# Cross-attention with a routed expert layer: seven maxima blocks for eight, new orders of the matrix engine, the first bias on VectorE

## The chip, the cores and the metric

One core of one Trainium2 chip. The metric is the device time of one execution in microseconds (us). The engines are TensorE (PE; its weight loads are PEld), VectorE (DVE), ScalarE (ACT), GpSimd (POOL) and SyncE (SP), which here only issues DMAs. Each works through its own program in order and waits on semaphores.

## The reference

```python
# x (16, 224, 512), context (16, 750, 384); 16 heads of 32; 8 experts of width 256, top 2
x = x + cross_attention(layernorm(x), context)      # softmax(q k^T / sqrt(32)) v, then Wo, bo
n = layernorm(x)
logits = cosine(n, centroids) + n @ w_route.T
gates = softmax of the two largest logits
h = gelu(n @ w1[e] + b1[e], exact); y_e = h @ w2[e] + b2[e]
x = x + sum_e gates[e] * y_e
```

## The kernel before

**Attention.** A group is four heads of one batch element; there are 64 (`GROUPS`), four to a batch element, and a quarter (`first`, `second`, `third`, `fourth`) of each engine's program belongs to each of the four. In quarter g the matrix engine interleaves, in an order written out by hand (L1629 to L1769): the projections of Q and K for group g + 2, parts of V for the batch element, the maxima of the scores of group g + 1 (`score_for_max`, L1529), the scores of g in twelve pairs (`score`, L1551), their products with V (`values`, L1567, three steps), the denominators of g - 1 (L1584), and now and then the output projection, the transposes of x and y and the logits. The order of the shared PSUM banks `M` is computed from the same list (`misc_units`, L90).

The maxima: for every one of the 4 x 224 query rows of a group the maximum over 750 keys is needed ahead of the exponential. `score_for_max` multiplies a block of rows with all keys (two matmuls into the one buffer `X`), `maximum` (L1066) on VectorE reduces it. A block has 112 rows, so there are 8 (`XU`). `transpose_max` (L1544) turns the eight columns into rows, ScalarE negates them, a DMA puts them into `qst`, and `score` adds them by way of a row of ones.

Exponentials run on ScalarE into `pr` (two halves, L773); GpSimd adds the six key tiles in five steps (`add_step`, L478), and `denominators` sums over partitions. VectorE inverts (`invert`), ScalarE and VectorE split the result in a high and a low part, for the products of three (`split3`).

**Second layernorm.** `y_stats` (L1105) on VectorE; the reciprocal roots (of the variance and of the length) on GpSimd (`y_rsqrt`, L531, 16 instructions with `pow`); `y_apply` on ScalarE. `rsqrt` (L34) is the same root in 12 VectorE instructions, without `pow`.

**Weights of the experts.** Sixteen pieces are loaded by SP and split: ScalarE copies the high part, VectorE subtracts it (`w_part`, L1146), after groups 62 to 66 and once ahead of the table.

**Routing.** VectorE picks two experts for each token, computes slots (`place`), and builds with the matrix engine a table of token numbers for each slot (`find_columns`, `find_rows`). `table_done` lets the first gather start.

**Experts.** 63 tiles of 128 slots (`TILES`). GpSimd gathers the rows of tile i (`gather`) and adds the result to `out` (`add_rows`). On the matrix engine: `fold_x` (four transposes), `up` (one matmul of a row of ones with the two parts of b1, then twelve), `fold_h` (two transposes of the gelu's result), `down` (six). The loop's orders:

```
PE : fold_x(i+2)  up(i+1)    down(i)    fold_h(i+1)
ACT: x_high(i+2)  gelu(i+1)  h_high(i+1)  y_scale(i)
DVE: x_low(i+2)   y_bias(i)  (load of the expert number)  h_low(i+1)
```

`x_high` and `x_low` split x, `h_high` and `h_low` the hidden layer (`down` waits for `h_low`), `y_bias` adds b2 and `y_scale` applies the gate.

## Time and profile before

| | us |
|---|---|
| median of 3 runs | 1650.93 (1650.54 to 1652.68) |
| the profiled execution | 1648.43 |
| its span, first to last instruction | 1646.6 |
| PE booked | 1524.2 (93%) |
| DVE, ACT, POOL booked | 1030.6, 944.2, 1080.2 |
| mean granted clock of PE | 0.964 of full speed |

The attention lasts until about 1320 us, the expert loop begins at about 1403. An engine's booked time contains the drain of its instructions, so that a booked matrix engine is not one that streams. In a timeline, times are start and length in us; the idle time ahead of an instruction and what ended it stand in brackets.

### The profile page before, as it was taken

To read this page: it belongs to the slowest core of one execution; us is meant where nothing else is said; L and a number is where in the kernel's file an instruction comes from. 1 tells how busy PE (TensorE), PEld (TensorE's weight loads), DVE (VectorE), ACT (ScalarE), POOL (GpSimd) and SP (SyncE) were. 2 spreads that over 40 slices of the span, in tenths; PEclk is the share of its full clock that TensorE was granted. 3 is DMA by queue.
4 is the path that set the end of the run, shared out by engine and by line. 5 is a ranking of instruction groups with operands and counts; after the bars stand their busy time and mean duration, and the time that the engine had idled before them with its cause. 6 is when DMAs were issued, how large, how long until landed. Compare 5 with 4: busy or idle time off the path is not lost.

```text
span 1646.6 us, 33344 instructions
## 1 busy us (share of the span) xinstructions
PE 1524.2 (93%) x11534; PEld 1247.4 (76%) x11534; DVE 1030.6 (63%) x1475; ACT 944.2 (57%) x2055; POOL 1080.2 (66%) x931
## 2 busy tenths in 40 slices
PE   4899999999999999999999999999999743899997
PEld 4777777778787878787877877877777433798996
DVE  5556666666666676766666666666665568344443
ACT  4456666666666666666666666665665440455554
POOL 3366767676767677776676777777775740477675
PEclk9999999999999999999999999999999765899999
DMA  7556666666667676767666757676756733578785
GB/s 193 97 81 111 101 134 123 110 124 108 127 110 134 111 129 112 131 110 139 112 130 107 136 101 144 101 140 101 140 91 120 187 122 35 136 135 147 135 148 90
DMA packets 113394, 199.29 MB, mean 121 GB/s; under 512 B 20448, under 2 KB 49280, under 8 KB 113104
## 3 DMA queue, kind: packets, MB, share of 16 engines
q1 hardware_dynamic: 98992, 165.81, 54.4%
q0 software_dynamic: 14240, 31.35, 10.5%
q8 instruction: 98, 1.61, 0.5%
q14 instruction: 64, 0.52, 0.1%
HBM read 64.29 MB, written 38.66 MB: 63 GB/s over the span
## 4 chain that ended last, share of the span: by engine, by line
PE 86%; DVE 5%; ACT 3%; POOL 2%; issue 1%; DMA 1%; POOLq 0%; DVEq 0%; SPq 0%; ACTq 0%
PE M L320 12%; PE S L1563 12%; PE M L321 12%; PE M L322 12%; PE X L1540 11%; PE O L1579 10%; ACT pr L781 2%; PE M L1825 2%; PE X L1807 2%; PE X L1808 2%; PE X L1806 2%; PE M L1826 2%; PE M L1827 2%; PE M L1590 2%; PE S L1796 2%
## 5 line engine op out<-in xcount | busy, mean ns | idle before, releaser
L1072 DVE TENSOR_REDUCE mx<-X 112x1 f32<-112x752 f32 x512 | 480.6, 939 | 356.0 <-PE X L1540 353.9
L491 POOL TENSOR_TENSOR psum_p<-psum_p,pr 125x896 f32<-125x896 f32 x256 | 543.9, 2124 | 172.6 <-ACT pr L781 149.1
L781 ACT ACTIVATE pr<-S 125x448 f32<-125x448 f32 x768 | 395.0, 544 | 224.4 <-PE S L1563 216.6
L1563 PEld LDWEIGHTS S<-qst,kst 128*125 128x125 f32 x1536 | 234.7, 189 | 113.0 <-ACT pr L781 51.2
L1563 PE MATMUL S<-qst,kst 128*125 128x224 f32 x1536 | 287.3, 291 | 27.1 <-ACT pr L781 21.2
L1540 PE MATMUL X<-kh_s,q_own 128*112 128x376 f32 x1024 | 272.0, 347 | 8.4 <-DVE mx L1072 7.9
L1540 PEld LDWEIGHTS X<-kh_s,q_own 128*112 128x112 f32 x1024 | 153.9, 176 | 48.0 <-issue 26.8
L1579 PE MATMUL O<-pr,v 125*32 125x224 f32 x3072 | 188.6, 364 | 1.7 <-ACT pr L781 1.7
L488 POOL TENSOR_TENSOR psum_p<-pr 125x896 f32<-125x896 f32 x64 | 135.6, 2119 | 80.1 <-ACT pr L781 79.9
L475 POOL TENSOR_TENSOR ctx_l<-ctx_r,ctx_h 128x750 fp32r<-128x750 f32 x48 | 85.4, 1811 | 74.7 <-ACT ctx_h L696 74.7
L320 PE MATMUL M<-ctx_h,wk_h 128*128 128x376 f32 (+1 forms) x384 | 130.0, 339 | 0.0
L321 PE MATMUL M<-ctx_l,wk_h 128*128 128x376 f32 (+1 forms) x384 | 129.4, 337 | 0.0
L322 PE MATMUL M<-ctx_h,wk_l 128*128 128x376 f32 (+1 forms) x384 | 128.8, 335 | 0.0
L1579 PEld LDWEIGHTS O<-pr,v 125*32 125x32 f32 x3072 | 81.3, 110 | 62.3 <-issue 23.1
L662 POOL DMA_INDIRECT out<-y_out,table_t x63 | 99.9, 1586 | 41.4 <-ACT y_out L1003 23.3
L654 POOL DMA_INDIRECT xg<-rows_d,table_x x63 | 62.4, 990 | 86.3 <-DVE settled L1400 43.0
L320 PE MATMUL M<-wv_h,ctx_h 128*125 128x512 f32 x288 | 116.8, 405 | 0.0
L322 PE MATMUL M<-wv_h,ctx_l 128*125 128x512 f32 x288 | 113.6, 394 | 0.0
L321 PE MATMUL M<-wv_l,ctx_h 128*125 128x512 f32 x288 | 113.5, 394 | 0.0
L1079 DVE RECIPROCAL M<-M 128x224 f32<-128x224 f32 x64 | 99.8, 1559 | 21.7 <-PE M L1590 21.6
L738 ACT ACTIVATE q_own<-qh_s,own 128x224 fp32r<-128x224 f32 x256 | 102.6, 472 | 2.1
L1062 DVE SCALAR_TENSOR_TENSOR kl_s<-M,bk_s,kh_s 128x376 fp32r<-128x376 f32 (+1 forms) x128 | 77.0, 602 | 14.3 <-ACT kh_s L749 14.1
(222 smaller groups left out, 3005.1 us busy)
## 6 DMA issues: line engine op xcount, KB each, us to landing
kst<-kh_s SPq DMA_DIRECT2D x128, 375.0 KB, 7.3
kst<-kl_s SPq DMA_DIRECT2D x64, 375.0 KB, 10.4
ctx_r<-ctxT SPq DMA_DIRECT2D x48, 375.0 KB, 12.2
qst<-qh_s SPq DMA_DIRECT2D x128, 112.0 KB, 2.8
rows_d<-x_res SPq DMA_DIRECT2D x32, 448.0 KB, 10.6
w_l<-w SPq DMA_DIRECT2D x16, 512.0 KB, 7.0
x_ln<-x SPq DMA_DIRECT2D x17, 448.0 KB, 11.0
qst<-ql_s SPq DMA_DIRECT2D x64, 112.0 KB, 3.0
```

Of the source, the lines that this page charges most:

```text
L320: pe.matmul(out, lhs[0], rhs[0], start=first, stop=False)
L321: pe.matmul(out, lhs[0], rhs[1], start=False, stop=False)
L322: return pe.matmul(out, lhs[1], rhs[0], start=False, stop=last)
L488: pool.tensor_tensor(out=total, in0=tiles[0], in1=tiles[1], op=ALU.add).then_inc(sum_step, 1)
L491: pool.tensor_tensor(out=total, in0=total, in1=tiles[half], op=ALU.add).then_inc(sum_step, 1)
L662: pool.indirect_dma_start(out=out[:, :], out_offset=bass.IndirectOffsetOnAxis(ap=table_t[:, i:i + 1], axis=0), in_=y_out[:, i % YO, :], in ...
L738: act.activation(q_own[:, g % 2, j, :], qh_s[:, g % 2, :], ACT.Copy, scale=own[:, j:j + 1]).then_inc(own_done, 1)
L781: act.activation(pr[0:KP, (3 * g + p) % 2, j, :, :], S[0:KP, n % SB, 0:2 * NQ].rearrange("p (i n) -> p i n", i=2), ACT.Exp).then_inc(exp_d ...
L1072: dve.tensor_reduce(mx[0:QP, u:u + 1], X[0:QP, :, 0:HALF[0][1]], AX.XY, ALU.max).then_inc(max_done, 1)
L1540: last = pe.matmul(X[0:QP, i, 0:w], q_own[:, g % 2, j, QP * qt:QP * (qt + 1)], kh_s[:, g % 2, off:off + w], start=True, stop=True)
L1563: last = pe.matmul(S[0:KP, n % SB, NQ * h:NQ * (h + 1)], kst[:, i, j, o:o + KP], qst[:, i, j, :], start=True, stop=True)
L1579: last = pe.matmul(O[HD * j:HD * (j + 1), 0:NQ], v[0:KP, 2 * p + i, HD * j:HD * (j + 1)], pr[0:KP, (3 * g + p) % 2, j, i, :], start=(p == ...
```

## The change

- `XU` is 7: the rows of the four heads are taken as one row of 896 and cut in blocks of 128. All eighth calls of `score_for_max` and `maximum` go.
- The four orders of the matrix engine and `misc_units` are written anew. Two of the four are shown.
- The roots of batch elements 14 and 15 are computed on VectorE (`late_root`), with `rsqrt` twice. GpSimd's constants come one group later, and there are two fewer.
- The last group's denominators take three of the five additions and the two last exponential tiles directly.
- b1 is written to DRAM and read back as a broadcast to all partitions; VectorE adds it (`h_bias`) ahead of the gelu, and the matmul with ones goes.
- b2 is loaded after the last output projection, not after the table.
- The weight subtractions on VectorE are dealt out otherwise: 2 after group 63 (5 before), 4 after 64 (3), 4 after 66 (4), 3 behind the table (1 ahead of it).
- `hot_row` is a ring of three chunks, not four.
- The expert loop's orders are new on three engines; x is prepared three tiles ahead.

```diff
-XU = 8
+XU = GH * NQ // P
...
-LN_STEPS, Y_STEPS = 8, 16
+LN_STEPS, Y_STEPS, LATE_STEPS = 8, 16, 2 * RSQRT_STEPS + 3
+LATE = B - 2
...
+ROWS = 3 * CHUNK
...
+        def roots(b):
+            return Y_STEPS * min(b, LATE) + LATE_STEPS * max(0, b - LATE)
+
+        def shifted(b):
+            return roots(b) + (LN_STEPS if b < LATE else RSQRT_STEPS + 1)
...
-                    if not 0 <= g < GROUPS:
+                    if not 0 <= g < GROUPS or (g == GROUPS - 1 and i >= 3):
...
-                        sp.wait_ge(zeroed, 1)
-                        sp.wait_ge(b1_hi, 1)
-                        sp.dma_start(b1_hl[0:1, :, :].bitcast(F32), b1_th[:, :].bitcast(F32)).then_inc(b1_both, 16)
-                        sp.wait_ge(b1_lo, 1)
-                        sp.dma_start(b1_hl[1:2, :, :].bitcast(F32), b1_tl[:, :].bitcast(F32)).then_inc(b1_both, 16)
+                        sp.wait_ge(b1_out, 1)
+                        sp.dma_start(b1_d[:, :], b1_t[:, :]).then_inc(b1_flat, 16)
                         sp.wait_ge(s_full, 12 * GROUPS)
                         load_pieces(E + 2, 2 * E)
+                        sp.wait_ge(b1_flat, 16)
+                        sp.dma_start(b1_all[:, :, :], b1_d.rearrange("(a e) p -> a (e p)", a=1).rearrange("a (e n) -> a e n", n=DE)
+                                     .broadcast_to([P, E, DE])).then_inc(b1_in, 16)
                     if t == 2 and b + 2 < B:
...
+                wait_full(sp, "O1", B - 1)
+                sp.dma_start(b2_all[:, :, :], b2.rearrange("(a e) n -> a e n", a=1).broadcast_to([P, E, D])
+                             ).then_inc(b2_in, 16)
                 sp.wait_ge(route, 15)
                 for i in range(2):
                     sp.dma_start(gates_of[i], gate4[0:QP, :, i, :]).then_inc(gate_out, 16)
-                sp.wait_ge(table_done, 1)
-                sp.dma_start(b2_all[:, :, :], b2.rearrange("(a e) n -> a e n", a=1).broadcast_to([P, E, D])
-                             ).then_inc(b2_in, 16)
-
                 sp.wait_ge(need_done, 1)
                 for i in range(1, TILES):
...
-                    if not 0 <= b < B:
+                    if not 0 <= b < LATE:
...
-                        act.wait_ge(sum_step, 5 * GROUPS)
-                        act.wait_ge(b1_both, 32)
+                        wait_full(act, "den", GROUPS - 1)
+                        act.wait_ge(b1_flat, 16)
...
-                    act.wait_ge(h_full, i + 1)
+                    act.wait_ge(h_read, i + 1)
                     if i >= 2:
                         act.wait_ge(ht_full, i - 1)
-                    act.activation(hid[:, i % 2, :], HP[:, i % 2, 0:DE], ACT.Gelu).then_inc(gelu_done, 1)
+                    act.activation(hid[:, i % 2, :], h_raw[:, i % 2, :], ACT.Gelu).then_inc(gelu_done, 1)
...
                 gelu(0)
+                x_high(2)
                 h_high(0)
                 for i in range(TILES):
-                    if i + 2 < TILES:
-                        x_high(i + 2)
                     if i + 1 < TILES:
                         gelu(i + 1)
+                    if i + 3 < TILES:
+                        x_high(i + 3)
+                    y_scale(i)
+                    if i + 1 < TILES:
                         h_high(i + 1)
-                    y_scale(i)
...
+                def late_root(b):
+                    n, m = roots(b), mv2[0:QP, :, :]
+                    v, y, tmp, off = ve2[0:QP, :], rstd2[0:QP, :], rtmp2[0:QP, :], shift2[0:QP, :]
+                    sq, ln = square[0:QP, :], length[0:QP, :]
+                    dve.wait_ge(y_var, QT * (b + 1))
+                    dve.wait_ge(yn_done, QT * b)
+                    rsqrt(dve, newton2, n, m[:, :, 1], EPS, ALU.add, v, y, tmp)
+                    n += RSQRT_STEPS
+                    dve.scalar_tensor_tensor(out=off, in0=m[:, :, 0], scalar=-1.0, in1=y, op0=ALU.mult,
+                                             op1=ALU.mult).then_inc(newton2, 1)
+                    wait_free(dve, "lg1", b - 1)
+                    dve.tensor_tensor(out=sq, in0=m[:, :, 1], in1=y, op=ALU.mult).then_inc(newton2, 1)
+                    dve.wait_ge(newton2, n + 2)
+                    dve.scalar_tensor_tensor(out=sq, in0=sq, scalar=float(D), in1=y, op0=ALU.mult,
+                                             op1=ALU.mult).then_inc(newton2, 1)
+                    dve.wait_ge(newton2, n + 3)
+                    rsqrt(dve, newton2, n + 3, sq, NORM_EPS2, ALU.max, v, ln, tmp)
+
...
+                    if b >= LATE:
+                        late_root(b)
...
-                        dve.wait_ge(b1_hi, 1)
-                        dve.tensor_tensor(out=b1_tl[:, :], in0=HP[0:2 * E, 0, 0:P], in1=b1_th[:, :],
-                                          op=ALU.subtract).then_inc(b1_lo, 1)
-                        for n in range(3, E):
+                        for n in range(3, 5):
                             w_part(n)
                     if g == GROUPS:
-                        for n in range(E, E + 3):
+                        for n in range(5, E + 1):
                             w_part(n)
                     if g == GROUPS + 2:
-                        dve.wait_ge(made, 8)
+                        dve.wait_ge(made, 7)
                         dve.tensor_scalar(upper[:, :], iota[:, :], float(DUMP + 1), lane[:, 0:1], ALU.add,
                                           ALU.is_gt).then_inc(masks, 1)
-                        dve.wait_ge(newton2, Y_STEPS * B)
-                        for n in range(E + 3, 2 * E - 1):
+                        for n in range(E + 1, E + 5):
...
-                w_part(2 * E - 1)
...
+                for n in range(E + 5, 2 * E):
+                    w_part(n)
...
+                def h_bias(i, e):
+                    dve.wait_ge(h_full, i + 1)
+                    if i >= 2:
+                        dve.wait_ge(gelu_done, i - 1)
+                    dve.tensor_tensor(out=h_raw[:, i % 2, :], in0=HP[:, i % 2, 0:DE], in1=b1_all[:, e, :],
+                                      op=ALU.add).then_inc(h_read, 1)
...
                 x_low(0)
                 e = expert_of(0)
                 x_low(1)
+                dve.wait_ge(b1_in, 16)
+                h_bias(0, e)
+                x_low(2)
                 h_low(0)
                 dve.wait_ge(b2_in, 16)
                 for i in range(TILES):
-                    if i + 2 < TILES:
-                        x_low(i + 2)
+                    if i + 1 < TILES:
+                        after = expert_of(i + 1)
+                        h_bias(i + 1, after)
+                    if i + 3 < TILES:
+                        x_low(i + 3)
                     y_bias(i, e)
                     if i + 1 < TILES:
-                        e = expert_of(i + 1)
                         h_low(i + 1)
+                        e = after
...
                         return
-                    j, qt = u // QT, u % QT
+                    own_q = q_own[:, g % 2, :, :].rearrange("p j n -> p (j n)")
                     if u == 0:
                         pe.wait_ge(kh_done, 2 * (g + 1))
-                    if qt == 0:
-                        pe.wait_ge(own_done, GH * g + j + 1)
+                    pe.wait_ge(own_done, GH * g + (P * (u + 1) - 1) // NQ + 1)
                     if g or u:
                         pe.wait_ge(max_done, XU * g + u)
                     for i, (off, w) in enumerate(HALF):
-                        last = pe.matmul(X[0:QP, i, 0:w], q_own[:, g % 2, j, QP * qt:QP * (qt + 1)],
+                        last = pe.matmul(X[:, i, 0:w], own_q[:, P * u:P * (u + 1)],
                                          kh_s[:, g % 2, off:off + w], start=True, stop=True)
                     last.then_inc(x_full, 1)
...
-                    pe.wait_ge(sum_step, 5 * (g + 1))
-                    for j in range(GH):
-                        last = pe.matmul(out[HD * j:HD * (j + 1), 0:NQ], ones[0:KP, :], psum_p[0:KP, g % 2, j, :],
-                                         start=True, stop=True)
+                    parts = [psum_p[0:KP, g % 2, :, :]]
+                    if g == GROUPS - 1:
+                        pe.wait_ge(sum_step, 5 * g + 3)
+                        pe.wait_ge(exp_done, 12 * (g + 1))
+                        parts += [pr[0:KP, (3 * g + 2) % 2, :, h, :] for h in range(2)]
+                    else:
+                        pe.wait_ge(sum_step, 5 * (g + 1))
+                    for n, part in enumerate(parts):
+                        for j in range(GH):
+                            last = pe.matmul(out[HD * j:HD * (j + 1), 0:NQ], ones[0:KP, :], part[:, j, :],
+                                             start=n == 0, stop=n == len(parts) - 1)
                     last.then_inc(full, 1)
...
                 def third(g, b):
                     project_q(g + 2)
                     score_for_max(g + 1, 0)
+                    values(g - 1, 2)
+                    score_for_max(g + 1, 1)
                     project_k(g + 2, 0)
-                    score_for_max(g + 1, 1)
-                    score(g, 0)
-                    values(g - 1, 2)
-                    score(g, 1)
-                    score_for_max(g + 1, 2)
-                    project_k(g + 2, 1)
-                    score(g, 2)
-                    score_for_max(g + 1, 3)
                     project_v(b + 1, 0, 0)
                     project_v(b + 1, 0, 1)
+                    score(g, 0)
+                    score_for_max(g + 1, 2)
+                    score(g, 1)
+                    score(g, 2)
+                    project_k(g + 2, 1)
                     score(g, 3)
+                    score_for_max(g + 1, 3)
+                    score(g, 4)
+                    score(g, 5)
                     denominators(g - 1)
+                    values(g, 0)
                     score_for_max(g + 1, 4)
                     project_v(b + 1, 1, 0)
-                    score(g, 4)
-                    score(g, 5)
                     project_v(b + 1, 1, 1)
                     score_for_max(g + 1, 5)
-                    values(g, 0)
                     score(g, 6)
+                    score(g, 7)
                     score_for_max(g + 1, 6)
-                    score(g, 7)
                     score(g, 8)
                     score(g, 9)
-                    score_for_max(g + 1, 7)
                     values(g, 1)
                     score(g, 10)
                     transpose_max(g + 1)
...
                 def fourth(g, b):
                     score_for_max(g + 1, 0)
                     project_q(g + 2)
+                    project_k(g + 2, 0)
+                    score_for_max(g + 1, 1)
                     values(g - 1, 2)
-                    score_for_max(g + 1, 1)
-                    project_k(g + 2, 0)
+                    score(g, 0)
                     score_for_max(g + 1, 2)
-                    score(g, 0)
                     score(g, 1)
                     project_k(g + 2, 1)
+                    score_for_max(g + 1, 3)
                     score(g, 2)
-                    score_for_max(g + 1, 3)
+                    score(g, 3)
+                    project_v(b + 1, 2, 0)
                     denominators(g - 1)
-                    project_v(b + 1, 2, 0)
-                    score(g, 3)
                     project_v(b + 1, 2, 1)
+                    score(g, 4)
+                    project_v(b + 1, 3, 0)
+                    score(g, 5)
+                    project_v(b + 1, 3, 1)
                     score_for_max(g + 1, 4)
-                    score(g, 4)
-                    score(g, 5)
-                    project_v(b + 1, 3, 0)
-                    project_v(b + 1, 3, 1)
-                    score_for_max(g + 1, 5)
                     score(g, 6)
                     score(g, 7)
+                    score_for_max(g + 1, 5)
                     values(g, 0)
-                    score_for_max(g + 1, 6)
-                    values(g, 1)
                     score(g, 8)
                     score(g, 9)
                     transpose_y(b - 1, 0)
                     transpose_y(b - 1, 1)
-                    score_for_max(g + 1, 7)
+                    score_for_max(g + 1, 6)
+                    values(g, 1)
                     score(g, 10)
                     transpose_max(g + 1)
                     score(g, 11)
...
-                        pe.wait_ge(gelu_done, i - 1)
+                        pe.wait_ge(h_read, i - 1)
                     h = HP[:, i % 2, 0:DE]
-                    pe.matmul(h, ones_r[:, :], b1_hl[:, e, :], start=True, stop=False)
                     for c in range(DC):
-                        pe.matmul(h, xTs[:, 0, i % 2, c, :], w1_h[:, e, c, :], start=False, stop=False)
...
-                pe.wait_ge(b1_both, 32)
-                pe.wait_ge(ew_lo, W_PIECES)
                 fold_x(0)
                 fold_x(1)
                 e = expert_of(0)
                 up(0, e)
+                fold_x(2)
                 fold_h(0)
                 for i in range(TILES):
-                    if i + 2 < TILES:
-                        fold_x(i + 2)
                     if i + 1 < TILES:
                         after = expert_of(i + 1)
                         up(i + 1, after)
+                    if i + 3 < TILES:
+                        fold_x(i + 3)
                     down(i, e)
                     if i + 1 < TILES:
                         fold_h(i + 1)
...
```

## Rows read from the trace of the kernel before

**Rows 1.** The page, chain that ended last, by engine

```profile
PE 86%; DVE 5%; ACT 3%; POOL 2%; issue 1%; DMA 1%; POOLq 0%; DVEq 0%; SPq 0%; ACTq 0%
```

**Rows 2.** Stretches, sum over one batch element: us, then booked us of each engine

```profile
sum 79.26, PE 78.01 PEld 62.82 DVE 52.66 ACT 49.47 POOL 56.35; mean PE 19.50 PEld 15.71 DVE 13.16 ACT 12.37 POOL 14.09
```

**Rows 3.** Chain in order of time, 700 to 704 us: start, us, what

```profile
701.02 0.43 PE S L1563 x4
701.46 0.89 PE O L1579 x16
...
702.76 0.34 PE X L1540 x2
```

**Rows 4.** Timeline of PE, end of a fourth quarter

```profile
764.19 0.57 PE L1540 MATMUL X<-kh_s,q_own 128*112 128x376 f32 x2
...
765.92 0.26 PE L1549 MATMUL M<-id_s,mx 112*8 112x112 f32 x1
```

**Rows 5.** Timeline of PE, one tile of the expert loop

```profile
1560.30 0.36 PE L1804 MATMUL X<-b_hl,ones_r 128*128 x1
1560.50 0.27 PE L1806 MATMUL X<-w_h,xTs 128*128 x1
...
1561.92 0.39 PE L1825 MATMUL M<-w_h,hTs 128*128 x1
...
1563.90 0.36 PE L1804 MATMUL X<-b_hl,ones_r 128*128 x1
```

**Rows 6.** Timelines of DVE, ACT and PE, pairs of instructions that follow one another

```profile
1560.03 0.69 DVE L1420 TENSOR_TENSOR y_raw<-M,b_all 128x512 f32<-128x512 f32 x1 [0.95 <-PE M L1827]
1560.69 0.42 DVE L1409 TENSOR_TENSOR hTs<-M,hTs 128x256 fp32r<-128x256 f32 x1
...
1563.63 0.69 DVE L1420 TENSOR_TENSOR y_raw<-M,b_all 128x512 f32<-128x512 f32 x1 [0.94 <-PE M L1827]
...
1565.60 0.69 DVE L1404 TENSOR_TENSOR xTs<-S,xTs 128x512 fp32r<-128x512 f32 x1 [0.54 <-ACT xTs L983]
...
1564.36 0.72 ACT L1003 ACTIVATE y_out<-y_raw,xg 128x512 f32<-128x512 f32 x1 [0.23 <-DVE y_raw L1420]
1564.99 0.58 ACT L983 ACTIVATE xTs<-S 128x512 fp32r<-128x512 f32 x1
...
1410.37 0.39 ACT L996 ACTIVATE hTs<-O 128x256 fp32r<-128x256 f32 x1 [0.78 <-PE O L1816]
...
1410.79 0.42 DVE L1409 TENSOR_TENSOR hTs<-O,hTs 128x256 fp32r<-128x256 f32 x1 [3.94 <-ACT hTs L996]
...
1636.82 0.42 DVE L1409 TENSOR_TENSOR hTs<-O,hTs 128x256 fp32r<-128x256 f32 x1
...
1637.37 0.47 PE L1825 MATMUL M<-w_h,hTs 128*128 x1 [1.14 <-DVE hTs L1409]
```

**Rows 7.** Waits, whole span: who waited for what, us in total, times, longest

```profile
DVE hTs L1409 <- issue: 7.6, 16, 1.0
```

**Rows 8.** Chain in order of time, between the loops

```profile
1307.56 1.08 POOL ve L539
...
1315.92 2.07 POOL psum_p L488
...
1321.51 8.20 DVE w_l L1149 x4
...
1395.90 7.29 DMA xg<-rows_d,table_x
```

**Rows 9.** Timeline of DVE, the root of the centroids' lengths

```profile
17.30 1.71 DVE L46 SCALAR_TENSOR_TENSOR ctmp<-ctmp,cve 8x1 f32<-8x1 f32 x1
19.04 0.15 DVE L47 SCALAR_TENSOR_TENSOR cinv<-ctmp,cinv 8x1 f32<-8x1 f32 x1
```

**Rows 10.** Stretches of 5 us: booked us (x instructions) of PE, PEld, DVE, ACT, POOL; PEclk, DMA

```profile
1280.00:1285.00 5.00, 3.05 (x17) 2.10 (x16) 3.47 (x4) 1.45 (x4) 5.00 (x4) 1.00 0.02 5
1285.00:1290.00 5.00, 4.22 (x27) 2.68 (x28) 0.99 (x2) 1.77 (x4) 2.68 (x2) 0.66 0.87 164
```

137 lines of the change are left out of this document (72 added, 65 removed).

## The prediction

> **What bounds the kernel now.** I read the stretches first, then the chain, then each engine's timeline. The chain that ended last runs for 86% of its length over the matrix engine [rows 1]. In a steady batch of the attention (four groups, 79.3 us) that engine is booked for 78.0 us [rows 2], and in the expert loop its instructions follow one another without a gap [rows 5]. So its instruction stream sets both loops; VectorE (52.7 of 79.3) and GpSimd (56.4) have room. Booked is not streaming, though: the timeline has the transpose of the maxima 1.73 us after the last maxima block (two matmuls of `score_for_max`), although only a score pair stands between them [rows 4]. There is one buffer `X`, and a block can't be followed by anything that needs its reduction before that time. Between the loops, from about 1282 to 1403 us, chains over VectorE, GpSimd and DMA decide.
>
> **Attention: eight maxima blocks become seven.** The same 896 query rows go through in blocks of 128 instead of 112. Each group loses one block of two matmuls of 376 columns, 0.34 us on the matrix engine [rows 3]; 63 of the 64 groups lie where it is the bound: 63 x 0.34 = 21 us. VectorE also loses a reduction, worth nothing by itself. The Trainium skill (TensorE: Matmul & The Clock Gate, Back-to-back issue gap) gives 376 / 2.4 + 2.5 = 159 ns a matmul, so 20 us here; the row has 170, so the trace nearly agrees.
>
> **New orders.** What they change is the distance between maxima blocks. A score pair takes 0.21 us and a value step 0.89 [rows 3]. In the third quarter before, three score pairs stand between two blocks: 0.34 + 0.63 = 0.97 us against 1.73, 0.8 us idle; in the fourth, one pair stands ahead of the transpose: 0.55 against 1.73, 1.2 us idle [rows 3, 4]. The new fourth puts a value step there and loses nothing; but it has two score pairs alone between blocks 4 and 5, and the new third between 5 and 6: 0.34 + 0.42 = 0.76 against 1.73, so 0.9 to 1.0 us twice, and `values` alone between blocks 0 and 1 of the third, another 0.3 to 0.5. Old idle about 2.0 us a batch, new 2.1 to 2.4: a tie, and I take zero. Its bounds are the whole idle time removed, 16 batches x 0.8 = -13 us, and half of the saving lost, +10. Attention: -21, from -34 to -11.
>
> **The first bias on VectorE.** The matmul with ones goes out of `up`. It holds 0.20 us of the 3.60 us of a tile [rows 5], so 3.40 are left (1.42 of them `up`). If the matrix engine stayed the bound, that would be -62 x 0.20 = -12 us. It doesn't stay the bound, because two engines get a new order. ScalarE now has gelu(i+1), x_high(i+3), y_scale(i), h_high(i+1); before, h_high(i+1) stood ahead of y_scale(i). VectorE has h_bias(i+1), x_low(i+3), y_bias(i), h_low(i+1). Engines work in program order, so h_high(i+1) is queued behind y_scale(i), which waits for y_bias(i), which waits for down(i); and down(i+1) waits for h_low(i+1), which waits for h_high(i+1). I follow that ring from start to start with the lags of the trace [rows 5, 6]:
> down(i) to y_bias(i) 1.71; to y_scale(i) 0.73; to the next ScalarE instruction 0.63; h_high to h_low 0.42; h_low to down(i+1) 0.55. Sum 4.04 us, more than the 3.60 of now. Before, the ring left out the middle pair: 1.71 + 0.66 + 0.55 = 2.92, and was hidden.
> A second ring needs no matrix engine, because all eight instructions of the two engines alternate: h_bias to gelu 0.46 (its 0.42, by h_low of the same width, and the 0.04 that y_bias to y_scale shows beyond 0.69); gelu to x_high 0.30 (0.39 less the 0.1 by which y_scale's successor starts before its end); x_high to x_low 0.61; x_low to y_bias 0.66 (as y_bias to h_low); y_bias to y_scale 0.73; y_scale to h_high 0.63; h_high to h_low 0.42; h_low to the next h_bias 0.38 (0.42 less the same overlap that y_bias to h_low shows). Sum 4.19 us [rows 6].
> In that last step VectorE also loads the expert's number into a register. Now the load stands behind y_bias, whose 0.66 us cover it except in 16 of the 63 tiles, which waited 7.6 us in all [rows 7]. Behind h_low only 0.38 cover it: 0.12 us a tile at least, and at most 0.28 more. I take 0.18 in all: 4.37 us a tile. From that 62 x (4.37 - 3.60) = +48 us; the ends are 4.04 (+27) and 4.60 (+62). Prefetching three tiles ahead instead of two gives nothing where these rings decide. GpSimd's gather and scatter of a tile keep pace with 3.60 us now and so with more.
>
> **Between the loops.** (a) `y_rsqrt(14)` and the constants leave GpSimd, where they stand for 8.4 us ahead of the last group's sums [rows 8]. Two of the last group's five additions go as well: its denominators take the third pair of exponentials directly, for 8 more short matmuls. Perfectly used, this and the four weight subtractions of 2.05 us that hold up `invert(63)` [rows 8] are worth about 10 us. (b) But the roots go to VectorE as a chain of 27 small instructions, 21 of them with two SBUF operands, ahead of three weight subtractions and of `invert(62)`; behind that stands `o_hi(62)` on ScalarE, and behind it the exponentials of the last group. Beside GpSimd's subtractions such a tiny instruction (8x1) took 1.71 us, where others of its kind took 0.15 [rows 9]. The Trainium skill says so (GPSIMD Engine Reference, Key points): GpSimd shares its SBUF interfaces with VectorE, in contention with two-input instructions. The trace agrees by those rows, and it speaks against this move. GpSimd's sums of group 62 end at 1307.5 us [rows 8]; with four or five such stalls until then and 0.2 us (0.15 and the hand-over) for each of the other steps, the chain takes 4 x 1.7 + 17 x 0.2 = about 10 us. VectorE has some 2 us to spare there, by my estimate, so `invert(62)` comes some 8 us later, and most of the gain of (a) is eaten: I take -3 us, between -9 and +4. The root of batch 15 meets an idle GpSimd: 13 steps of 0.2 us to the shift, against 2.7 us now, no change. (c) One weight subtraction leaves the chain ahead of the table and three go behind it, under the first gather: -1 (0 to -2). (d) `b2` (2 MB) is no longer issued with the first gather, which took 7.3 us [rows 8]: -1.5 (0 to -3). (e) The first bias goes through DRAM and back as a broadcast, far ahead of the loop; three row buffers instead of four and the shorter waits are hidden by PE's own work there. Sum -5.5, from -14 to +4.
>
> **The sum.** -21 + 48 - 5.5 = +21.5 us on the profiled execution's 1648.4 us: 1670. The median of the runs shown is 2.5 us above it; I leave the forecast at 1670.
>
> **Rivals.** (A) The loop of experts stays with the matrix engine, as if y_scale found its data early: 3.40 to 3.60 us a tile. Then 1648.4 - 21 - 5.5 - 6 = 1616. Against it: y_scale starts 0.73 us after y_bias, which starts 1.71 after down, as the rows have it [rows 5, 6]. That leaves an error in my reading of the orders, or buffers that let the engines drift; 12%.
> (B) The rings are as short as their lower end, 4.04 us, and the new orders of the attention take out all idle time: -34 + 27 - 9 = -16, 1632. It is faster than before, the other side from my forecast, and is decided by whether the second ring's VectorE part (h_bias behind h_low, x_low ahead of y_bias) is really serial. 7% for a result below 1647.
> (C) Attention and transition give nearly as much as the rings take: within 0.2%; 5%.
> (D) The gap of about a microsecond in each tile costs clock: from 1280 to 1285 us the engine was booked for 3.05 of 5 us, and in the next 5 us the granted clock was 0.66 of full speed, so partly at 1.2 GHz instead of 2.4 [rows 10]. In the loop it would be at work for 3.40 of 4.37 us. A tile at the lower level holds up to 6.8 us of matrix work, 2.4 more than the ring; one tile in six so would be 10 x 2.4 = +24, 1694. 12%.
> Forecast itself: 64%, its own range 1648 to 1692.
>
> **Numbers.** 1670 us; the range that leaves no more than 2 in 10 out: 1630 to 1698. Faster by over 0.2% (3.3 us, about what a measurement can tell from no change) 0.19, same 0.05, slower 0.76.
>
> **What would show it.** Right: down to down 4.2 to 4.6 us in the expert loop, matrix engine waiting for h_low there, ScalarE's y_scale directly ahead of h_high with no idle time of note on VectorE or ScalarE; a batch of the attention at 77.9 us (1.4 less), with waits of PE for `mx` between score pairs of the third and fourth quarter; in the transition small root instructions of 1.7 to 2.1 us on VectorE. Wrong: tiles at 3.4 to 3.6 us (the rings are not closed), a batch under 77 us (orders worth more than the block), a transition shortened by over 10 us (no contention).

## The result, and the profile after it

The changed kernel takes 1692.36 us (median of 4 runs, 1691.41 to 1694.39), the one before 1651.44 us beside it (4 runs): ratio 1.0242, 95% interval 1.0228 to 1.0255, slower by 41 us. The forecast was 1670, with a range of 1630 to 1698: the sign and the mechanism of the loop were right, the size of the loss was put at half of what it is. The page's header, its chain by engine (it answers to [rows 1]) and its clock:

```profile
span 1690.5 us, 33260 instructions
...
PEclk9999999999999999999999999999997659999999
...
PE 64%; DVE 12%; issue 11%; ACT 6%; POOL 4%; DVEq 1%; DMA 1%; ACTq 0%; POOLq 0%; SPq 0%
```

The matrix engine's part of the chain fell from 86 to 64%; VectorE's rose from 5 to 12%, and "issue", time in which an engine waited for nothing that the profile shows, from 1 to 11%. The two spans, 1646.6 and 1690.5 us, cut at marks that both timelines have (the transposes of the maxima, and the first matmul of each tile's `down`):

| stretch | before, us | after, us | difference | forecast |
|---|---|---|---|---|
| start to the last transpose of maxima (attention) | 1299.0 | 1284.3 | -14.7 | -21 |
| to the first `down` (between the loops) | 113.7 | 109.2 | -4.5 | -5.5 |
| first to last `down` (62 tiles) | 224.7 | 287.8 | +63.1 | +48 |
| to the end | 9.2 | 9.2 | 0 | 0 |
| sum | 1646.6 | 1690.5 | +43.9 | +21.5 |

So the loop of experts is the whole loss: 4.64 us a tile (median 4.61) where it was 3.62. The timelines of VectorE, then of ScalarE, then of the matrix engine, for one tile of it (start, us of work, engine, line, what, in brackets the idle time ahead and who ended it); they answer to [rows 5, 6]:

```profile
1504.26 0.42 DVE L1450 TENSOR_TENSOR hTs<-O,hTs 128x256 fp32r<-128x256 f32 x1 [1.06 <-ACT hTs L1014]
1505.08 0.42 DVE L1445 TENSOR_TENSOR h_raw<-X,b_all 128x256 f32<-128x256 f32 x1 [0.39 <-issue]
1506.47 0.69 DVE L1438 TENSOR_TENSOR xTs<-S,xTs 128x512 fp32r<-128x512 f32 x1 [0.97 <-ACT xTs L1001]
1507.08 0.68 DVE L1461 TENSOR_TENSOR y_raw<-M,b_all 128x512 f32<-128x512 f32 x1
1508.82 0.42 DVE L1450 TENSOR_TENSOR hTs<-M,hTs 128x256 fp32r<-128x256 f32 x1 [1.06 <-ACT hTs L1014]
1509.76 0.42 DVE L1445 TENSOR_TENSOR h_raw<-X,b_all 128x256 f32<-128x256 f32 x1 [0.51 <-issue]
```

```profile
1505.54 0.42 ACT L1008 ACTIVATE hid<-h_raw 128x256 f32<-128x256 f32 x1 [1.31 <-DVE h_raw L1445]
1505.86 0.58 ACT L1001 ACTIVATE xTs<-S 128x512 fp32r<-128x512 f32 x1
1507.80 0.72 ACT L1021 ACTIVATE y_out<-y_raw,xg 128x512 f32<-128x512 f32 x1 [1.36 <-DVE y_raw L1461]
1508.42 0.36 ACT L1014 ACTIVATE hTs<-M 128x256 fp32r<-128x256 f32 x1
```

```profile
1504.82 0.47 PE L1873 MATMUL M<-w_h,hTs 128*128 x1 [0.39 <-DVE hTs L1450]
...
1509.38 0.47 PE L1873 MATMUL M<-w_h,hTs 128*128 x1 [0.40 <-DVE hTs L1450]
```

Read the first two side by side and the second ring of the forecast stands there, each instruction started by the one before it on the other engine: `h_bias` 1505.08, `gelu` 1505.54, `x_high` 1505.86, `x_low` 1506.47, `y_bias` 1507.08, `y_scale` 1507.80, `h_high` 1508.42, `h_low` 1508.82, the next `h_bias` 1509.76. Both engines idle for over half of the time (VectorE is booked for 110 of 240 us, ScalarE for 97, below), each waiting for the other in turn, and the matrix engine waits for `h_low` in every tile. The lags are 0.46, 0.32, 0.61, 0.61, 0.72, 0.62, 0.40 and 0.94 us. The waits of the whole span say the same of all tiles (us in total, times, longest); the second line answers to [rows 7]:

```profile
DVE hTs L1450 <- ACT hTs L1014: 65.8, 62, 1.1
...
DVE h_raw L1445 <- issue: 30.3, 61, 1.0
...
PE M L1873 <- DVE hTs L1450: 26.8, 62, 2.2
...
PE X L1854 <- issue: 16.1, 61, 0.4
```

"issue" ahead of `h_raw` is VectorE's register load of the expert's number, and what `h_bias` itself has to pass behind it: half a microsecond in 61 tiles, where [rows 7] have it in 16 for 7.6 us. The granted clock of the whole stretch was 1.00, the level of 2.4 GHz, with the matrix engine booked for 205 of 240 us (columns: stretch, length, busy us and count of PE, PEld, DVE, ACT and POOL, clock, DMA share, GB/s):

```profile
1420.00:1660.00 240.00, 205.21 (x1231) 164.43 (x1230) 109.90 (x206) 96.93 (x205) 132.23 (x103) 1.00 0.62 109
```

In the attention, a steady batch (stretches, sum; it answers to [rows 2]) and the matrix engine's timeline at the two places that the forecast named (third quarter, blocks 5 to 6; fourth, blocks 4 to 5) and at the fourth's transpose, which answers to [rows 4]:

```profile
sum 78.31, PE 76.00 PEld 62.07 DVE 47.01 ACT 48.68 POOL 56.26; mean PE 76.00 PEld 62.07 DVE 47.01 ACT 48.68 POOL 56.26
```

```profile
812.90 0.50 PE L1586 MATMUL X<-kh_s,q_own 128*128 128x376 f32 x2
813.24 0.59 PE L1609 MATMUL S<-qst,kst 128*125 128x224 f32 x4
814.52 0.58 PE L1586 MATMUL X<-kh_s,q_own 128*128 128x376 f32 x2 [0.70 <-DVE mx L1092]
...
830.18 0.51 PE L1586 MATMUL X<-kh_s,q_own 128*128 128x376 f32 x2
831.82 0.59 PE L1586 MATMUL X<-kh_s,q_own 128*128 128x376 f32 x2 [0.69 <-DVE mx L1092]
...
834.47 0.59 PE L1586 MATMUL X<-kh_s,q_own 128*128 128x376 f32 x2
...
836.20 0.27 PE L1595 MATMUL M<-id_s,mx 128*7 128x128 f32 x1
```

Ahead of the last line, the transpose, nothing is idle any more: the value step fills the time. Two waits of 0.7 us stand where the forecast put 0.9 to 1.0.

### The profile page after: what moved, and what is told of

Same layout as the page of the kernel before. It is cut to its first block, busy times and chain, and to the rows that moved or that the text cites. A ratio compares the mean times of both kernels' runs of the same rounds, so it can differ in the third digit from the quotient of the medians.

```text
span 1690.5 us, 33260 instructions
## 1 busy us (share of the span) xinstructions
PE 1512.7 (89%) x11359; PEld 1229.2 (73%) x11359; DVE 975.4 (58%) x1527; ACT 926.2 (55%) x2055; POOL 1062.6 (63%) x895
## 4 chain that ended last, share of the span: by engine, by line
PE 64%; DVE 12%; issue 11%; ACT 6%; POOL 4%; DVEq 1%; DMA 1%; ACTq 0%; POOLq 0%; SPq 0%
PE M L343 11%; PE M L345 11%; PE M L344 11%; PE S L1609 10%; PE X L1586 9%; PE O L1625 8%; POOL psum_p L513 3%; DVE y_raw L1461 2%; DVE mx L1092 2%; PE M L1643 2%; ACT pr L799 2%; DVE h_raw L1445 1%; ACT hTs L1014 1%; DVE hTs L1450 1%; ACT xTs L1001 1%
## 5 line engine op out<-in xcount | busy, mean ns | idle before, releaser
L1092 DVE TENSOR_REDUCE mx<-X 128x1 f32<-128x752 f32 x448 | 421.1, 940 | 441.7 <-PE X L1586 440.2
L513 POOL TENSOR_TENSOR psum_p<-psum_p,pr 125x896 f32<-125x896 f32 x254 | 537.1, 2115 | 179.5 <-ACT pr L799 156.6
L799 ACT ACTIVATE pr<-S 125x448 f32<-125x448 f32 x768 | 385.7, 543 | 222.5 <-PE S L1609 192.8
L1609 PEld LDWEIGHTS S<-qst,kst 128*125 128x125 f32 x1536 | 241.9, 190 | 89.5 <-ACT pr L799 42.3
L1586 PE MATMUL X<-kh_s,q_own 128*128 128x376 f32 x896 | 241.4, 351 | 31.9 <-DVE mx L1092 27.4
L1586 PEld LDWEIGHTS X<-kh_s,q_own 128*128 128x128 f32 x896 | 145.3, 191 | 68.8 <-issue 49.4
L1625 PE MATMUL O<-pr,v 125*32 125x224 f32 x3072 | 183.9, 361 | 2.5 <-ACT pr L799 2.5
L1625 PEld LDWEIGHTS O<-pr,v 125*32 125x32 f32 x3072 | 85.3, 110 | 59.9 <-issue 18.1
L344 PE MATMUL M<-wv_l,ctx_h 128*125 128x512 f32 x288 | 113.7, 395 | 0.0
L1021 ACT ACTIVATE y_out<-y_raw,xg 128x512 f32<-128x512 f32 x63 | 45.6, 724 | 87.2 <-DVE y_raw L1461 80.4
```

The source lines that it names most:

```text
L344: pe.matmul(out, lhs[0], rhs[1], start=False, stop=False)
L513: pool.tensor_tensor(out=total, in0=total, in1=tiles[half], op=ALU.add).then_inc(sum_step, 1)
L799: act.activation(pr[0:KP, (3 * g + p) % 2, j, :, :], S[0:KP, n % SB, 0:2 * NQ].rearrange("p (i n) -> p i n", i=2), ACT.Exp).then_inc(exp_d ...
L1092: dve.tensor_reduce(mx[:, u:u + 1], X[:, :, 0:HALF[0][1]], AX.XY, ALU.max).then_inc(max_done, 1)
L1586: last = pe.matmul(X[:, i, 0:w], own_q[:, P * u:P * (u + 1)], kh_s[:, g % 2, off:off + w], start=True, stop=True)
L1609: last = pe.matmul(S[0:KP, n % SB, NQ * h:NQ * (h + 1)], kst[:, i, j, o:o + KP], qst[:, i, j, :], start=True, stop=True)
```

## The experiments

Four questions: is it the ring, and what is its register load worth; what bounds the loop once the ring is open; where the attention's saving stayed; and what the move of the roots costs. All kernels are the changed one with an edit, except where the text says that the base is the kernel before. Ratios are to the kernel before, on the same chip; where fewer than four runs stand behind a time, their number is given.

### The ring: `e1_gate_last`, `e2_load_early`, `e3_both`

The first gives ScalarE the order of before for two instructions:

```diff
-                    y_scale(i)
                     if i + 1 < TILES:
                         h_high(i + 1)
+                    y_scale(i)
```

> The changed kernel with one line moved: on ScalarE h_high(i+1) stands ahead of y_scale(i) again. Theory (two closed rings set the expert loop): without y_scale both rings open; what is left is h_bias to gelu 0.46, to x_high 0.32, to x_low 0.61, to y_bias 0.61, to h_low 0.65, and 0.88 to the next h_bias with its register load = 3.53 us a tile instead of 4.64, so 62 x 1.11 = 69 us less: about 1624 us. Rival (the loop is slow because the bias went to VectorE at all, or because of the prefetch three tiles ahead, and the place of y_scale is immaterial): 4.4 to 4.6 us a tile, 1680 to 1692 us.

Measured: 1636.96 us (2 runs), ratio 0.9903 (0.9875 to 0.9932), 3.765 us a tile (median 3.64). Two lines exchanged are worth 55 us: with `h_high(i+1)` ahead of `y_scale(i)` neither ring closes. The tile isn't at 3.53 us, though, as was expected.

The second moves only VectorE's register load, to behind `y_bias(i)`, an expert earlier:

```diff
                     if i + 1 < TILES:
-                        after = expert_of(i + 1)
                         h_bias(i + 1, after)
...
                     y_bias(i, e)
+                    e = after
+                    if i + 2 < TILES:
+                        after = expert_of(i + 2)
```

> The changed kernel with only VectorE's load of the expert number moved: the number of tile i+2 is loaded behind y_bias(i), not ahead of h_bias(i+1). Theory (the register load costs about 0.5 us in every tile when only 0.38 us of h_low cover it): h_low to h_bias falls from 0.82 to 0.94 us to 0.38, the ring to 4.64 - 0.50 = 4.14 us, 62 x 0.5 = 31 us less: about 1661 us. Rival (the gap ahead of h_bias is not the load but a wait for the matrix engine's up): no change, 1690 to 1694 us.

Measured: 1661.16 us (4 runs), ratio 1.0042 (1.0017 to 1.0066), 4.10 us a tile, as expected (1661 us, 4.14). The ring is whole here, but from `h_low` to `h_bias` it takes 0.34 us instead of 0.82 to 0.94. VectorE's timeline of this kernel:

```profile
1506.14 0.42 DVE L1450 TENSOR_TENSOR hTs<-M,hTs 128x256 fp32r<-128x256 f32 x1 [1.06 <-ACT hTs L1014]
1506.48 0.41 DVE L1445 TENSOR_TENSOR h_raw<-X,b_all 128x256 f32<-128x256 f32 x1
```

The ring without the load is 4.10 us (forecast 4.19), the load adds 0.54 (forecast 0.18). This settles the term that was mis-sized.

The third has both edits:

> Both edits. Theory: no ring over 3.2 us is left, the matrix engine is the bound again with 3.40 us a tile, or up to 3.7 if its own register load ahead of up stays visible (it waited 0.3 us there in the changed kernel): 62 x 0.95 to 1.25 = 59 to 77 us less, 1615 to 1633 us. Rival (the bias on VectorE costs the loop something by itself): over 3.75 us a tile, over 1637 us.

Measured: 1637.54 us, ratio 0.9907 (0.9878 to 0.9936), 3.73 us a tile, no different from the first. That lies between the 3.70 us of the theory and the 3.75 of the rival, and decides between them no more than the time does. So the two cures don't add up: with the ring open VectorE has time for its load, and something else holds the tile at 3.7 us. A candidate was the matrix engine's own register load between `fold_h` and `up` ("PE X L1854 <- issue" in the waits above, of the change). In this kernel, too, the start of `up` lies later behind the last transpose of `fold_h` than it need: 0.17 us by the median and up to 0.58 in nine tiles of ten, where it is 0.03 in the kernels that have that load elsewhere.

### What bounds the open loop: `e5_loads`, `e10_pe_load`

`e5_loads` is `e3_both` with that load put where the matrix engine has queued work, behind `fold_x(i + 3)` and ahead of `down`, an expert earlier:

```diff
                     if i + 1 < TILES:
-                        after = expert_of(i + 1)
                         up(i + 1, after)
                     if i + 3 < TILES:
                         fold_x(i + 3)
-                    down(i, e)
+                    e = after
+                    if i + 2 < TILES:
+                        after = expert_of(i + 2)
+                    down(i, now)
```

> The kernel with both edits of the loop (gate scaling behind h_high, VectorE's load early), and the matrix engine's load of the expert number moved too: the number of tile i+2 is loaded behind fold_x(i+3), ahead of down(i), instead of between fold_h and up. Theory (the 0.3 to 0.6 us that the matrix engine idles between fold_h and up are this load): 3.40 to 3.50 us a tile instead of 3.73, 62 x 0.28 = 17 us less: about 1620 us. Rival (up waits there for something else, such as x_low): no change, 1634 to 1640 us.

Measured: 1626.54 us (2 runs), ratio 0.9872 (0.9842 to 0.9902); median tile 3.48 us, mean 3.59. The median is the 3.40 to 3.50 of the theory, the mean isn't. With the bias still on VectorE the loop is now faster than that of the kernel before, so the rival of `e3_both` (the bias costs the loop something by itself) falls as well. In its timeline the matrix engine has no wait over many tiles, and in the stretch below it is booked for 176.5 of 180 us (`e3_both` for 176.4, so that the booked share doesn't tell the two apart):

```profile
1420.00:1600.00 180.00, 176.47 (x1200) 158.28 (x1199) 103.64 (x201) 101.08 (x200) 127.14 (x99) 1.00 0.77 139
```

This is the state in which the removed matmul of 0.20 us counts: 3.61 us (median of before) became 3.48. What separates mean and median are seven tiles of 3.8 to 5.4 us. GpSimd's waits name a possible part of it: its scatter of a tile was held by SP seven times, 14.6 us in all. That this is what makes these tiles late isn't shown.

`e10_pe_load` leaves VectorE's load where the change put it and has the two other edits:

> The changed kernel with h_high ahead of y_scale and with the matrix engine's register load moved, but VectorE's register load left where the change put it, between h_low and h_bias. My theory: once the ring over y_scale is open, VectorE is no longer the bound and its load costs next to nothing: e1_gate_last's 3.765 us a tile less the 0.14 that the moved load of the matrix engine gave between e3_both and e5_loads, so 3.62 us, 1628 us. Rival: VectorE's four instructions and its load are themselves the bound as soon as the matrix engine's idle time is gone: no gain over e1_gate_last, 3.73 to 3.77 us, 1635 to 1637 us.

Measured: 1632.09 us (4 runs), ratio 0.9882 (0.9865 to 0.9898); 3.634 us a tile, median 3.48. The tile is as my theory had it (3.62), and not at the rival's 3.73 to 3.77; the time is 4 us above the theory's 1628. The same register load that cost 0.54 us a tile inside the ring costs 0.04 outside of it by the means and nothing by the medians (3.48 in both); `e9_loads_gaps` (below), which has the loop of `e5_loads` line for line, has a mean of 3.66, so that 0.04 isn't told from nothing. Of the 6.1 us between the profiled executions of `e10_pe_load` and `e5_loads`, 2.7 lie in the loop and 3.6 in the attention, where one of the last groups alone took 4.5 us more (below).

### Where the attention's saving stayed: `e4_gaps`, `e7_seven_old_orders`, `e8_old_orders_loads`, `e9_loads_gaps`

`e4_gaps` puts longer work between the maxima blocks that wait:

```diff
 in third:
-                    score_for_max(g + 1, 1)
                     project_k(g + 2, 0)
+                    score_for_max(g + 1, 1)
...
                     denominators(g - 1)
-                    values(g, 0)
                     score_for_max(g + 1, 4)
...
                     score(g, 7)
+                    values(g, 0)
                     score_for_max(g + 1, 6)
 in fourth:
-                    score_for_max(g + 1, 5)
                     values(g, 0)
+                    score_for_max(g + 1, 5)
```

> The changed kernel with three swaps in the matrix engine's orders of the attention: in the third quarter block 1 stands behind project_k and values(g, 0) between the score pairs 6, 7 and block 6; in the fourth values(g, 0) stands ahead of block 5. No two blocks are then closer than 1.4 us of work. Theory (these three places idle 0.4, 0.7 and 0.7 us a batch because X is still read by the reduction): 1.3 to 1.8 us less a batch, 16 batches, 20 to 29 us less: about 1668 us. Rival (the matrix engine would wait for exponentials or GpSimd's sums instead): under 6 us less, 1686 to 1692 us.

Measured: 1686.43 us, ratio 1.0203 (1.0173 to 1.0232): 6 us less than the change. A batch takes 78.06 us (sum of the four quarters' medians; 78.55 in the change), 0.5 less and not 1.3 to 1.8. The timelines of the matrix engine and of VectorE in the third quarter show why:

```profile
807.01 0.58 PE L1586 MATMUL X<-kh_s,q_own 128*128 128x376 f32 x2 [0.43 <-DVE mx L1092]
```

```profile
804.03 1.57 DVE L1099 RECIPROCAL M<-M 128x224 f32<-128x224 f32 x1
805.63 0.39 DVE L1106 TENSOR_TENSOR o_s<-o_s,M 128x224 f32<-128x224 f32 x1
805.93 0.93 DVE L1092 TENSOR_REDUCE mx<-X 128x1 f32<-128x752 f32 x1
```

The reduction of block 4 is now queued behind the reciprocal and the product of another group, 2 us, so block 5 waits for it. A gap filled in the matrix engine's order opened one in VectorE's, which I had not laid beside it. Over 700 to 860 us, two batches, the waits for the maxima are down to 0.9 us from the 2.8 of the change (below), so 0.95 a batch were won; half a microsecond of it goes to a wait that the change doesn't have, of the transposes of y for ScalarE:

```profile
PE M L1514 <- ACT x_res L830: 1.0, 2, 0.5
```

`e7_seven_old_orders` is the kernel before with seven blocks of 128 rows, its orders kept, block 7 left out of them:

```diff
-XU = 8
+XU = GH * NQ // P
...
 in each quarter:
-                    score_for_max(g + 1, 7)
```

> The kernel before with seven blocks of 128 rows and nothing else of the change: the eighth block's calls are struck out of the old orders. Theory (the new orders gave back part of what the block saved: idle time at the buffer X, which in the old orders stood mostly around block 7 of the third and fourth quarter, 0.7 and 1.2 us a batch, and goes with it): a batch of four groups takes 79.2 - 1.4 - 1.0 to 1.9 = 76 to 77 us, 16 batches, 35 to 50 us less than before: about 1608 us. Rival (the idle time moves to the score pairs and stays): 77.9 to 78.5 us a batch as in the changed kernel, 1630 to 1639 us.

Measured: 1637.45 us (3 runs), ratio 0.9935 (0.9896 to 0.9975). Counted over the same 60 groups (first transpose of maxima to the 61st): 1190.9 us before, 1180.7 here, 1177.9 in the change. The 0.34 us of a block, 20.4 us in 60 groups, are thus half kept with the old orders (5 of the 10 us in the first batch alone), and the new ones are worth 2.8 us more, where the seven kernels with the change's attention lie between 1177.8 and 1179.5. What takes up the other half here isn't the buffer `X`. The matrix engine's waits, in the same two batches (700 to 860 us), of the kernel before, of this one and of the change:

```profile
PE S L1563 <- ACT pr L781: 2.0, 4, 0.8
```

```profile
PE S L1558 <- ACT pr L781: 2.7, 4, 1.2
PE M L1585 <- POOL psum_p L491: 1.2, 3, 0.8
```

```profile
PE X L1586 <- DVE mx L1092: 2.8, 4, 0.7
PE S L1609 <- ACT pr L799: 0.9, 4, 0.3
PE X L1586 <- ACT q_own L756: 0.6, 2, 0.3
PE M L1643 <- POOL psum_p L513: 0.3, 1, 0.3
```

With the old orders the score pairs wait for ScalarE's exponentials and the denominators for GpSimd's sums: 3.9 us in two batches against 2.0 before, so 0.95 a batch more. Four blocks are 1.36 us; 1.36 - 0.95 leaves 0.4, and 0.5 was measured (79.22 to 78.73 us a batch by the quarters' medians). In the change the waits for the exponentials fall to 0.9 and those for the maxima and `q_own` come to 3.4, 4.6 us in all. By the same account only 0.1 us a batch would be left, where 0.7 is measured (78.55), so its orders also took out time to which no wait of before is put down: the matrix engine is booked for 76.0 us of a batch instead of 78.0 [rows 2], which is more than the 1.36 of the blocks.

The first of these lists has no wait of a matmul for the maxima (weight loads waited for them for 0.7 us in the two batches), and that bears on the forecast. Between the two lines of [rows 4] stands this one:

```profile
765.61 0.48 PE L1563 MATMUL S<-qst,kst 128*125 128x224 f32 x2 [0.84 <-ACT pr L781]
```

The idle time ahead of the transpose, which the forecast put down to the buffer `X`, stands ahead of a score pair that waits for one of ScalarE's exponentials. The reduction ended at 765.74 us, so the transpose couldn't have come much sooner either: the gap has two causes, and a block less takes away one of them.

`e8_old_orders_loads` has the old orders and the loop of `e5_loads`:

```diff
 e5_loads, in each quarter and in the planner's list:
-  the change's order
+  the order of before, without score_for_max(g + 1, 7)
```

> The changed kernel with the loop of e5 and the old orders of the attention less block 7. Theory (attention and expert loop are additive): the attention of e7 and the loop of e5, 1650 - 42 - 5 - 11 = about 1590 us. Rival (the old orders don't suit the changed kernel): the batch stays at 78.5 us, 1620 us.

Measured: 1635.01 us, ratio 0.9923 (0.9894 to 0.9952), against 1626.54 (0.9872) for `e5_loads`: neither my 1590 nor quite the rival. The 60 groups take 1183.3 us with the old orders and 1178.5 with the new. This fells the thought that the change's orders lose what the old ones would keep.

`e9_loads_gaps` adds the three swaps of `e4_gaps` to `e5_loads`:

> The three cures of the loop (as in e5_loads) together with the three swaps in the third and fourth quarter (as in e4_gaps). If the two add up, as they should, because they lie in different loops: a batch of the attention 0.5 us shorter, 8 us in all, and the loop at 3.59 us a tile: 1626.5 - 8 = 1619 us, ratio to the kernel before 0.981 to 0.983. If the swaps' saving falls among what other waits take up again: 1624 to 1627.

Measured: 1624.35 us (4 runs), ratio 0.9836 (0.982 to 0.9852), the fastest of all by its ratio, though the intervals of the two overlap. The 60 groups take 1172.4 us, 6.1 less than in `e5_loads`, as expected, but the profiled spans are equal (1625.8 and 1625.7): the last three groups give back 2.4 us and the loop 4 (a few more late tiles). The second last group is worth a look. In the seven kernels with the change's orders it takes from 19.25 to 23.80 us, here 20.65 and in `e4_gaps` 23.86. `e10_pe_load` is the one with 23.80; the matrix engine's timeline in it:

```profile
1257.11 0.45 PE L1609 MATMUL S<-qst,kst 128*125 128x224 f32 x2 [3.21 <-DMA qst<-mneg]
```

The score pair waits for the transfer of the maxima, which SP had issued at 1250.02, 7 us earlier. So the 3.6 us of attention between `e10_pe_load` and `e5_loads` are this group's, and `e4_gaps` lost in it over half of the 7.7 us that its swaps had gained in the 60 groups. It isn't the experts' weights that delay the maxima: the first of them is issued 23 us later,

```profile
1280.56 3.09 SPq L436 DMA_DIRECT2D w_l<-w  x3
```

What is under way are loads of x, of 448 KB each, issued at 1247.78 and 1248.14, and the copies of q and k. The second load of x lands 8.2 us after its issue, in `e5_loads`, where SP issues the same transfers in the same order, 5.5 us. Why the transfers are slower in one execution than in the other stays open.

### The roots: `e6_roots_pool`

```diff
-LATE = B - 2
+LATE = B
```

The last two batches' roots stay on GpSimd; all else is the change's.

> The changed kernel with LATE = B: all roots on GpSimd as before, nothing else. Theory (on VectorE the root of batch 14 is held up by GpSimd's additions and delays invert(62), and with it the last exponentials and ScalarE's eight weight copies behind them, more than its six us on GpSimd cost): last exponentials some 5 us earlier, about 6 us less: 1686 us. Rival (GpSimd's chain of additions decides, so that taking the roots off it was worth 6 us): 4 to 6 us more, 1697 us.

Measured: 1691.81 us (2 runs, 1688.73 and 1694.89), ratio 1.0268 (1.0216 to 1.032), the stretch between the loops 108.4 us against 109.2: no difference in the time. But two differences are in it that cancel. The timelines of VectorE, of the change (the same stretch of the transition) and then of this kernel; the last transpose of maxima, from which the times below are counted, is at 1284.3 us in the first and at 1288.2 in the second:

```profile
1283.94 1.18 DVE L41 TENSOR_SCALAR ve<-mv 112x2 f32<-112x2 f32 x1
...
1285.56 2.09 DVE L45 TENSOR_TENSOR rtmp<-rstd 112x2 f32<-112x2 f32 x1
1287.68 0.16 DVE L46 SCALAR_TENSOR_TENSOR rtmp<-rtmp,ve 112x2 f32<-112x2 f32 x1
1287.88 1.99 DVE L47 SCALAR_TENSOR_TENSOR rstd<-rtmp,rstd 112x2 f32<-112x2 f32 x1
...
1293.91 5.38 DVE L1189 TENSOR_TENSOR w_l<-w_l,w_h 128x1024 fp32r<-128x1024 f32 x3
1299.21 1.55 DVE L1099 RECIPROCAL M<-M 128x224 f32<-128x224 f32 x1
```

```profile
1291.19 1.65 DVE L1189 TENSOR_TENSOR w_l<-w_l,w_h 128x1024 fp32r<-128x1024 f32 x1 [3.42 <-ACT w_h L864]
...
1298.27 1.57 DVE L1099 RECIPROCAL M<-M 128x224 f32<-128x224 f32 x1 [1.25 <-PE M L1643]
```

The chain of roots of batch 14 takes 10 us on VectorE, with two stalls of 2.0 to 2.1 us and one of 1.2 (four or five of 1.7 were forecast). Without it `invert(62)` starts 10.1 us behind the last transpose instead of 14.9, so 4.9 us earlier, and the last exponentials end 4.8 us earlier, as the theory had it (5). The last output projection is still 4.8 us earlier. Then batch 15 takes the gain back. From its variance to `y_apply` it is 2.6 us in the change and 7.2 here, because GpSimd's first instruction of that root lasts as long as VectorE's four weight subtractions beside it:

```profile
1329.18 4.71 POOL L561 TENSOR_SCALAR ve<-mv 112x2 f32<-112x2 f32 x1 [15.49 <-DVE mv L1154]
```

```profile
1329.18 4.62 DVE L1189 TENSOR_TENSOR w_l<-w_l,w_h 128x1024 fp32r<-128x1024 f32 x4
```

The kernel before had VectorE wait for that root ahead of the subtractions (`dve.wait_ge(newton2, Y_STEPS * B)` in the diff); the change took that wait out, and this kernel doesn't put it back. So the run doesn't price the move of both roots against the order of before. It shows that batch 14's root costs 4.8 us on VectorE, and that batch 15's would cost 4.6 us on GpSimd without the wait; batch 14 on GpSimd and batch 15 on VectorE together wasn't run.

## Why the prediction was right in its sign and short in its size

**The ring, right.** The forecast followed the two engines' orders round and found a closed ring of eight instructions, 4.19 us with lags of the trace before; seven of its lags sum to 3.81 in the forecast and 3.74 in the trace after, and `e2_load_early` measured 4.10 for the whole. The first ring, 4.04, was the shorter of the two and didn't decide: from `down` to `y_bias` it has 2.26 us (1504.82 to 1507.08) instead of 1.71. `e1_gate_last` shows the cause by itself, 55 us for one exchange.

**The register load, wrong: the term that was mis-sized.** "I take 0.18 in all" became 0.54: 62 x 0.36 = 22 us too little. The ring itself was 0.09 us shorter than forecast, -6, which leaves 16; the loop fell short by 15 of the 22 us that the sum did. The forecast reasoned that if 0.66 us of `y_bias` nearly cover the load, then 0.38 us of `h_low` leave at most 0.28 of it more, 0.40 in all. From this range of 0.12 to 0.40 us it took 0.18, without a reason. The upper end for the tile, 4.60, was passed too. What the term lacked stands in the records of the load itself, of the change at 1504.3 us and of the whole kernel before (duration in ns: shortest, median, longest; first and last start in us):

```profile
L1455 DVEq TENSOR_LOAD <-which_i x1: 300/300/300, 1504.3 to 1504.3; - x1
```

```profile
L1414 DVEq TENSOR_LOAD <-which_i x63: 300/306/980, 1405.2 to 1636.2; - x63
```

The load does run beside the instruction ahead of it: it starts with `h_low` (1504.26). With the two steps that belong to it, of 0.19 and 0.02 us, it is through 0.60 us after that start, and `h_bias` has its own waits to pass behind it, 0.22 us more: 0.82 from start to start, of which `h_low` covers 0.42. Behind `y_bias`, before, the same load was through 0.61 us after the start, and `h_low` followed 0.05 later: 0.66, inside the 0.69 of `y_bias` [rows 6]. The 16 tiles of [rows 7] are those in which the load's record lasts 0.43 us or more instead of 0.30. So the forecast had the cover right and no length for what it covers. From the start of `h_low` to that of `h_bias` it is 0.92 us by the mean in the change and 0.34 without the load (`e2_load_early`).

**The eighth block, right in size, not in what it is worth.** The -21 us counted the matmuls as if a saved microsecond on a fully booked engine arrived whole. It was -13.0 us over 60 groups, -2.2 in the last three (these take 55.0 to 60.2 us in the kernels with the same orders) and +0.5 ahead of them. "A tie" between the idle times of the orders is the second step that failed: 7.4 of the 20.4 us in 60 groups didn't arrive, about 0.5 us a batch, 8 us in all, inside its stated bound of +10. Of its two sides the new one was near: the two places of 0.9 to 1.0 us were found at 0.70 and 0.69, the third, 0.3 to 0.5 us, at 0.30, which the trace puts down to `q_own`. The old one, 2.0 us a batch at `X`, had a second cause that the forecast didn't look at: the matmuls of two batches wait for ScalarE's exponentials and never for the maxima, and 0.84 of the 1.2 us read from [rows 4] is such a wait. But the idle times around `X` weren't all that decided: `e7_seven_old_orders` shows that with the orders unchanged, too, only 10 of 20 us arrive, since waits for ScalarE and GpSimd take up the time. The forecast looked at one buffer and one engine.

**Between the loops, right in sum.** -4.5 against -5.5. By parts, from milestones relative to the last transpose of maxima: to the last output projection -1.0 (forecast for (a) and (b) -3), to the start of the routing +0.7, to the end of the table -1.0 (c: -1), to the first `fold_x` -3.6 (d: -1.5, at most -3), to the first `down` +0.4 (not forecast). So the sum is right in part by luck: (a) and (b) gave 2 us less and (d) 2 us more than forecast. For (d), the first `fold_x` starts 3.8 us after GpSimd starts on the first gather (1379.89), where [rows 8] have 7.29 us for that gather alone; b2 was issued 45 us ahead of it instead of with it:

```profile
1383.68 1.09 PE L1845 MATMUL S<-id_s,xg 128*128 128x128 f32 x4 [6.22 <-DMA xg<-rows_d,table_x]
```

For (a) and (b), `invert(62)` came 5.3 us later than before by the same milestone (some 8 were forecast). `e6_roots_pool` shows the two apart: with the roots on GpSimd the last output projection would have been 5.8 us earlier than before, and batch 14's root on VectorE took 4.8 of it. In (b) the last group's `o_hi` is no longer held up by VectorE but by ScalarE's own eight copies of weights, which end at 1318.16 us with `o_hi` at 1318.07 behind them. The Trainium skill (GPSIMD Engine Reference, Key points) has VectorE's two-input instructions in contention with GpSimd; the trace agrees by the 2.09 and 1.99 us of 112x2 instructions that take 0.16 otherwise, in the time of two additions on GpSimd (1285.55 to 1289.85 us). `e6_roots_pool` shows it from the other side as well, with 4.71 us for one instruction of GpSimd.

**The rivals.** (A) and (B) fell with the timeline of the loop. (D), the clock, did not happen: 1.00 in the loop with 205 of 240 us booked. Had (D) been left out, nothing of the sum would differ.

## What to carry to other kernels

When two in-order engines hand work to each other several times in one iteration, write down their instructions alternately and follow the ring from start to start; an exchange of two neighbours can open or close it (here 55 us), and while it is closed nothing saved on the third engine arrives. Put register loads behind an instruction whose successor waits anyway: the same load cost 0.54 us a tile inside the ring and outside of it nothing that could be told from zero. Time saved on an engine that is booked for 98% isn't credited in full until each other engine's queue has been laid beside the new order; here half of it arrived. Before an idle time is put down to a buffer, read every line between its two ends. And a run that undoes a move has to put back the waits that guarded the old place, and is to be read by milestones too: two effects of nearly 5 us cancelled in `e6_roots_pool`.

## What the runs showed of the hardware

A load of a number from on-chip memory into a register starts beside the instruction ahead of it and is through about 0.6 us later (0.30 for the load's own record, up to 0.98 in some tiles). Behind an instruction of 0.69 us it was hidden in 46 of 62 tiles of the kernel before; behind one of 0.42 it left VectorE without work for 0.39 and 0.51 us, in 61 tiles, 30.3 us in all. On the matrix engine it is 16.1 us in 61 tiles, and moving it gave 0.14 us a tile (`e3_both` to `e5_loads`). Tiny instructions of VectorE took 2.0 us instead of 0.16 beside GpSimd's additions, and one of GpSimd's took 4.71 beside VectorE's subtractions (`e6_roots_pool`). The transfer of the maxima held up the matrix engine by 0.7 us in all near the end of the attention in `e5_loads` and by 3.9 in `e10_pe_load`, whose orders are the same there; a scatter of this size, up to 4.5 us in one group, is larger than several of the effects looked for here.
